# Another order of one attention step on four engines, a null key padded to 128 rows, and a VectorE copy of half of the mixed heads

## The reference, cut to what matters

```python
q = (xn @ Wq).reshape(b, n, HEADS, DIM_HEAD).transpose(0, 2, 1, 3)   # 16 heads of 64
kv = xn @ Wkv                                                       # one key and value for all heads
k = jnp.concatenate([nk, k], axis=1)                                # a null key in front: 129 keys
v = jnp.concatenate([nv, v], axis=1)
q = l2norm(q) * q_scale
k = l2norm(k) * k_scale
sim = jnp.einsum('bhid,bjd->bhij', q, k) * SCALE
sim = sim + attn_bias                                               # relative position and null bias
sim = jnp.where(causal, neg, sim)
attn = jax.nn.softmax(sim, axis=-1)
out = jnp.einsum('bhij,bjd->bhid', attn, v)
out = out.transpose(0, 2, 1, 3).reshape(b, n, HEADS * DIM_HEAD)
return ln(out @ Wout, g_out)
```

## Time and profile before

| what | value |
|---|---|
| median of 3 runs | 434.51 us |
| profiled execution, own time | 434.13 us |
| its span, first to last instruction | 432.0 us |
| busy share of the span, PE / DVE / ACT / POOL | 83% / 68% / 65% / 53% |
| mean granted TensorE clock | 0.929 |
| chain that ended last, by engine | PE 60%, DVE 16%, POOL 7%, issue 7%, ACT 5%, DMA 4% |
| attention steps 3 to 15 | 81 us to 231 us of the span |

### The profile page before, as it was taken

How to read it: one execution, slowest core, us unless ns; L and a number is a source line. 1 busy time by engine, 2 the same in 40 slices (tenths; PEclk the granted TensorE clock), 3 DMA queues, 4 the chain that set the end, 5 groups by cost and what they waited for, 6 DMA issues and landing times.

```text
span 432.0 us, 10178 instructions
## 1 busy us (share of the span) xinstructions
PE 357.3 (83%) x2921; PEld 295.1 (68%) x2922; DVE 292.6 (68%) x1144; ACT 279.5 (65%) x935; POOL 229.2 (53%) x253
## 2 busy tenths in 40 slices
PE   0286776999999999999998989697619999999980
PEld 0275655677777777777776648496519999999980
DVE  1848385888888888888889894757305565566545
ACT  1385594999999999999996773464304444444440
POOL 5024843678876667667872552277730444344420
PEclk9998995999999999999999687869958999999997
DMA  6726299990000000000000000011121222111117
GB/s 185 204 80 200 67 212 191 202 163 2 2 2 2 3 2 2 3 0 2 3 2 2 1 2 0 14 50 58 49 56 26 63 61 61 49 56 55 35 58 236
DMA packets 39479, 26.55 MB, mean 61 GB/s; under 512 B 4464, under 2 KB 37130, under 8 KB 39438
## 3 DMA queue, kind: packets, MB, share of 16 engines
q1 hardware_dynamic: 34256, 20.60, 21.8%
q0 software_dynamic: 2240, 4.23, 2.9%
q10 hardware_dynamic: 2942, 1.21, 1.1%
HBM read 12.89 MB, written 13.54 MB: 61 GB/s over the span
## 4 chain that ended last, share of the span: by engine, by line
PE 60%; DVE 16%; POOL 7%; issue 7%; ACT 5%; DMA 4%; SPq 1%; ACTq 0%; DVEq 0%; POOLq 0%
PE bank L1188 45%; PE bank L1185 14%; POOL sent_rows L537 7%; DVE p_space L1014 2%; ACT p_space L687 2%; DMA q_space<-in_L_cond_g_dram 2%; DVE biasm_space L1140 1%; DVE xn L934 1%; DMA bias<-result_rows 1%; DVE low L1018 1%; DVE p_space L841 1%; ACT xn L610 1%; DVE GL L918 1%; ACT yh L779 1%; DVE norm_in L812 1%
## 5 line engine op out<-in xcount | busy, mean ns | idle before, releaser
L687 ACT ACTIVATE p_space<-p_space,low 128x129 f32<-128x129 f32 x256 | 99.0, 391 | 6.4 <-DVE low L1018 6.4
L502 POOL TENSOR_TENSOR p_space<-p_space,inv 128x516 f32<-128x516 f32 x64 | 67.1, 1049 | 66.1 <-DVE inv L1026 66.1
L1014 DVE SCALAR_TENSOR_TENSOR p_space<-bank,rn,biasm_space 128x129 f32<-128x129 f32 x256 | 72.0, 343 | 22.3 <-PE bank L1188 22.0
L493 POOL TENSOR_TENSOR biasm_space<-bias,madd 128x516 f32<-128x516 f32 x64 | 75.6, 1192 | 7.4 <-DVE p_space L1014 7.3
L543 POOL DMA_INDIRECT result_rows<-oT_space,dest_ring x38 | 37.6, 990 | 60.8 <-DVE dest_ring L1154 60.1
L768 ACT ACTIVATE biasm_space<-bank 128x384 f32<-128x384 f32 x54 | 26.6, 492 | 58.1 <-PE bank L1185 58.0
L1185 PE MATMUL bank<-ident,p_space 128*128 128x128 f32 (+1 forms) x272 | 48.5, 297 | 2.4 <-POOL p_space L502 2.1
L687 ACT ACTIVATION_READ_ACCUMULATOR p_space<-p_space,low 128x1 f32 x256 | 48.5, 190 | 0.0
L1188 PE MATMUL bank<-DT,biasm_space 128*128 (+1 forms) x324 | 46.4, 281 | 1.2 <-ACT biasm_space L768 1.2
L702 ACT ACTIVATE pT<-bank 128x512 f32<-128x512 f32 x64 | 37.3, 583 | 13.9 <-PE bank L1188 12.8
L1018 DVE TENSOR_REDUCE low<-p_space 128x4 f32<-128x516 f32 x64 | 44.2, 691 | 2.2
(11 more groups left out here) (217 smaller groups left out, 705.4 us busy)
## 6 DMA issues: line engine op xcount, KB each, us to landing
sent_rows<-fill_row SPq DMA_DIRECT2D x2, 1950.0 KB, 24.1
sent_rows<-fill_row SPq DMA_DIRECT2D x2, 1885.0 KB, 19.6
q_space<-sent_rows SPq DMA_DIRECT2D x38, 65.0 KB, 1.9
xs<-in_x_dram SPq DMA_DIRECT2D x4, 256.0 KB, 6.3
bias<-bias_rows SPq DMA_DIRECT2D x1, 1024.0 KB, 5.8
xn<-result_rows SPq DMA_DIRECT2D x4, 256.0 KB, 4.4
bias<-result_rows SPq DMA_DIRECT2D x4, 256.0 KB, 5.6
out_dram<-xs SPq DMA_DIRECT2D x4, 256.0 KB, 2.5
```

Source lines behind the costliest of these rows:

```text
L493: nc.gpsimd.tensor_tensor(biasm[:, b % 2, heads, :], bias[:, heads, :], madd[:, b:b + 1, :].to_broadcast([P, HC, KEYS]), ALU.add).then_inc ...
L502: nc.gpsimd.tensor_tensor(v, v, spread(inv[:, b % 2, heads], KEYS), ALU.mult).then_inc(p_normed, 1)
L687: last = nc.scalar.activation(v, v, ACT.Exp, bias=low[:, b % 2, h:h + 1], accum_out=den[:, b % 2, h:h + 1])
L1014: last = nc.vector.scalar_tensor_tensor(Pb[:, q, h, :], src, rn[:, q, h:h + 1], biasm[:, q, h, :], ALU.mult, ALU.add)
```

## The change

Six edits. (1) TensorE's step has another order: `mix(2)` moves to the next step, in front of `mix(3, 3)`; `scores(3)` follows `scores(2)`; `turn_pn` goes in front of `turn_p(3)`, and `turn_sums` comes last. (2) The first half of the mixed heads is copied by VectorE, a new `keep_oT` between `invert(1, 1)` and `scores(3)`; ScalarE keeps the second half. The semaphore `oT_kept` becomes `oT0_kept` and `oT1_kept`. (3) ScalarE's `keep_q(1)` goes in front of `keep_pT(1)`, and `keep_pn` in front of `keep_pT(3)`. (4) VectorE's `invert(3, 2)` goes in front of `scores(1)`. (5) GpSimd's step has another order, and chunks 2 and 3 of the masked bias are made for batches t and t-1 instead of t-2. (6) `null_out` and `pnT` have 128 rows, zeroed by two memsets at the start, so that the null key's matmul contracts over 128 rows.

The diff, without the declarations of semaphores and tiles (and with the calls in the steps):

```diff
@@ gpsimd @@
+            nc.gpsimd.memset(null_out[:, :], 0.0).then_inc(const_made, 1)
+            nc.gpsimd.memset(pnT[:, :], 0.0).then_inc(const_made, 1)
...
                 norm_p(2, 3)
-                add_mask(2, 2)
+                norm_p(3, 3)
+                norm_p(0, 2)
                 add_mask(0, 0)
-                norm_p(3, 3)
-                add_mask(3, 2)
-                norm_p(0, 2)
+                norm_p(1, 2)
+                add_mask(3, 1)
+                add_mask(2, 0)
                 add_mask(1, 0)
-                norm_p(1, 2)
@@ scalar @@
-                        nc.scalar.activation(pnT[:, :], bank[4][0:H, 0:P][:, ::-1], ACT.Copy).then_inc(pn_kept, 1)
+                        nc.scalar.activation(pnT[0:H, :], bank[4][0:H, 0:P][:, ::-1], ACT.Copy).then_inc(pn_kept, 1)
...
-                def keep_oT(g, back):
-                    if on(back):
-                        b = t - back
-                        act.wait_ge(mixed, NCH * b + 2 * (g + 1))
+                def keep_oT():
+                    if on(3):
+                        b = t - 3
+                        act.wait_ge(mixed, NCH * b + 4)
                         need(act, y_made, b - 1)
...
-                keep_oT(1, 3)
+                keep_oT()
...
+                keep_q(1)
                 keep_pT(1)
-                keep_q(1)
...
-                keep_oT(0, 2)
+                keep_pn()
                 keep_pT(3)
-                keep_pn()
@@ vector @@
+                def keep_oT():
+                    if on(2):
+                        b = t - 2
+                        dve.wait_ge(mixed, NCH * b + 2)
+                        need(dve, y_made, b - 1)
+                        nc.vector.tensor_copy(oT[:, p, 0:HALF * P].rearrange("p (k s) -> p k s", k=HALF),
+                                              bank[6][:, :].rearrange("p (k s) -> p k s", k=HALF)[:, :, ::-1]).then_inc(oT0_kept, 1)
...
                 scores(0)
+                invert(3, 2)
                 scores(1)
-                invert(3, 2)
...
+                keep_oT()
                 scores(3)
@@ tensor @@
                         if c % 2 == 0:
-                            need(pe, oT_kept, 2 * b + c // 2)
+                            need(pe, oT1_kept if c == 0 else oT0_kept, b + c // 2)
...
-                        pe.wait_ge(oT_kept, 2 * (t - 2))
+                        pe.wait_ge(oT0_kept, t - 2)
+                        pe.wait_ge(oT1_kept, t - 2)
...
                 queries(0)
                 turn_p(0)
+                mix(2, 3)
                 mix(3, 3)
...
                 scores(2, 1)
+                scores(3, 1)
                 mix(1, 2)
                 sum_squares()
...
+                turn_pn()
                 turn_p(3)
-                scores(3, 1)
                 turn_sums()
...
-                turn_pn()
-                mix(2, 2)
```

More of the change, by code:

```diff
@@ L50, in adaln_ffn_kernel @@
     CHAIN = 11
-    CONSTS = 23
+    CONSTS = 25
     MLP0_DMAS, MLP_DMAS, ROW_DMAS, SCALE_DMAS, EXPERT_DMAS = 3, 5, 3, 5, 5
@@ L113, in adaln_ffn_kernel @@
         vsel = sb("vsel", [P, QT, H])
-        null_out = sb("null_out", [H, D])
+        null_out = sb("null_out", [P, D])
         bias = sb("bias", [P, H, KEYS])
@@ L155, in adaln_ffn_kernel @@
         pT = sb("pT", [P, 2, HC * P])
-        pnT = sb("pnT", [H, P])
+        pnT = sb("pnT", [P, P])
         o_space = sb("o_space", [P, 2 * HD])
@@ L247, in adaln_ffn_kernel @@
             "biasm_made", "scored", "biased", "maxed", "exped", "inv_made", "p_normed"))
-        p_turned, p_kept, pn_turned, pn_kept, mixed, oT_kept, y_made, y_kept = (sem(n) for n in (
-            "p_turned", "p_kept", "pn_turned", "pn_kept", "mixed", "oT_kept", "y_made", "y_kept"))
+        p_turned, p_kept, pn_turned, pn_kept, mixed, oT0_kept, oT1_kept, y_made, y_kept = (sem(n) for n in (
+            "p_turned", "p_kept", "pn_turned", "pn_kept", "mixed", "oT0_kept", "oT1_kept", "y_made", "y_kept"))
         yh_made, yl_made, gate_made, up_made, silu_made, h_made, h_turned, hT_kept, down_made, down_kept, fin_made = (
@@ L649, in _ @@
             act.wait_ge(null_turned, 1)
-            nc.scalar.activation(null_out[:, :], bank[7][0:H, 0:D], ACT.Copy).then_inc(null_kept, 1)
+            nc.scalar.activation(null_out[0:H, :], bank[7][0:H, 0:D], ACT.Copy).then_inc(null_kept, 1)
             def keep_yT(g):
@@ L707, in keep_sums @@
                         nc.scalar.activation(sums_sb[:, :], bank[7][:, 0:P], ACT.Copy).then_inc(sums_kept, 1)
-                def keep_oT(g, back):
-                    if on(back):
-                        b = t - back
-                        act.wait_ge(mixed, NCH * b + 2 * (g + 1))
+                def keep_oT():
+                    if on(3):
+                        b = t - 3
+                        act.wait_ge(mixed, NCH * b + 4)
                         need(act, y_made, b - 1)
-                        nc.scalar.activation(oT[:, b % 2, g * HALF * P:(g + 1) * HALF * P].rearrange("p (k s) -> p k s", k=HALF),
-                                             bank[6][:, :].rearrange("p (k s) -> p k s", k=HALF)[:, :, ::-1], ACT.Copy).then_inc(oT_kept, 1)
+                        nc.scalar.activation(oT[:, q, HALF * P:2 * HALF * P].rearrange("p (k s) -> p k s", k=HALF),
+                                             bank[6][:, :].rearrange("p (k s) -> p k s", k=HALF)[:, :, ::-1], ACT.Copy).then_inc(oT1_kept, 1)
                 if t == NB + 1:
@@ L1433, in step @@
                     expert_across(LATE[3])
-                turn_pn()
-                mix(2, 2)
             run_steps(pe, step)
-            pe.wait_ge(oT_kept, 2 * NB)
+            pe.wait_ge(oT0_kept, NB)
+            pe.wait_ge(oT1_kept, NB)
             expert_regs = [pe.alloc_register(f"expert_reg{k}") for k in range(RING + 2)]
```

## The result

| what | before | after |
|---|---|---|
| median of the timed runs | 434.25 us | 446.16 us |
| ratio, with its 95% interval | | 1.028 [1.025, 1.031] |
| profiled execution, own time | 434.13 us | 446.81 us |
| its span | 432.0 us | 445.0 us |
| one middle step, from `project` to `project` | 12.04 us | 12.75 us |

The account below looks back on a forecast made before the run. The prediction took TensorE to bound the kernel before, and VectorE with GpSimd after. Holds, the copy and the end summed to +17.3 us on 434.13, giving 451 us, range 438 to 464.

Parts of the forecast that it names:

- The mechanism: In `norms`, VectorE links with two SBUF inputs starting inside GpSimd's adds wait for the pass: two or three of about 1.1 us per step.
- The walk: Timing from the start of invert(1,1) in a middle step: GpSimd's adds end at 5.03 us, holding the norm chain 1.85 us.
- TensorE's pause: Before `project` in each middle step, TensorE waits about 1.7 us for VectorE's norm result.
- VectorE's step: Middle steps: 10.4 us plus 0.6 copy plus 1.85 hold, about 12.8 us, bounds 12.55 and 13.2.
- The copy: The copy moved to VectorE adds 0.6 us of work, with no wait in a full step.
- TensorE at 11.1 us: Middle steps: six fewer changes of matmul shape at 0.16 us each, so TensorE needs 11.1 us instead of 12.04.
- The clock rival: TensorE's granted clock falls in the new pauses of the middle steps: 465 us, or part of it, chance 0.18.
- The rival that the holds do not decide: The schedule drifts until GpSimd's adds miss the links, and TensorE's gain of 0.95 us per step counts: 424 us, chance 0.10.
- The rival of one hold per step: One held link per step instead of two and a half, VectorE's step 12.0 us: about 438 us, chance 0.12.
- The early steps: Steps 0, 1 and 2: holds, plus the copy in step 2, add 1.9, 3.0 and 2.2 us.
- The end: Step 14's root for y gains 0.9 us; step 17's `choose`, behind the VectorE copy, costs 2.0 us.
- The root's -0.9: In step 14 one GpSimd add no longer runs beside the root for y, saving 0.9 us.

Follow-up runs that it names:

- experiment 1: The changed kernel with GpSimd's order of before put back: 424.15 us, ratio 0.978.
- experiment 4: The changed kernel with two `add_mask` passes instead of three between GpSimd's norm passes of chunks 1 and 2: 434.38 us, ratio 1.003.
- experiment 9: The changed kernel with one `add_mask` pass between those norm passes and the other adds placed to wait for nothing late: 424.38 us, ratio 0.975.
- experiment 6: The changed kernel with the norm chain's handed-on values in PSUM and two products per Newton step swapped: 418.35 us, ratio 0.964.
- experiment 3: The changed kernel with both copies of the mixed heads on ScalarE, none on VectorE: 442.02 us, ratio 1.023.
- experiment 8: The kernel before with the null key padded to 128 rows and nothing else: 428.28 us, ratio 0.988.
- experiment 2: The kernel before with GpSimd's new order alone: 451.09 us, ratio 1.043.
- experiment 10: The changed kernel with the norm chain's values in PSUM and step 17's first-half copy on ScalarE: 415.16 us, ratio 0.956.
- experiment 11: The changed kernel with the norm chain's values in PSUM, step 17's first-half copy on ScalarE and GpSimd's order of before: 417.19 us, ratio 0.960.
- experiment 5: The changed kernel with two `add_mask` passes moved behind GpSimd's norm pass of chunk 3, leaving one behind that of chunk 1: 444.12 us, ratio 1.024.
- experiment 7: The changed kernel with GpSimd's order of before and, in step 17 alone, the first-half copy on ScalarE: 419.40 us, ratio 0.967.

## Why the prediction was right

It said 451 us (438 to 464), slower at 0.79; the measured 446.16 lies in the range and beyond 2%, and at the low edge of the forecast's own 446 to 456. By its steps:

- **The mechanism** was right and is shown: links that start inside GpSimd's adds, two per step at 1.11 us. The walk gave a hold of 1.85, the trace has 1.88; it had the first exposed link delayed by 0.04 and two held fully, and so it is. TensorE's pause came to 1.42 us, where 1.7 was said. Experiments 1, 4 and 9 move the adds away one by one and the hold goes with them; experiment 6 leaves them and takes away the SBUF operand.
- **VectorE's step**: 12.8 predicted, 12.75 measured; steps 3 to 14 +9.1 against +8.97.
- **The copy** at 0.6: it holds VectorE 0.58 (175.36 to 175.94), with no wait ahead of it in a full step, and experiment 3 shows that its length does not count while the adds set the end.
- **TensorE** at 11.1 us: 11.09 in experiment 1, and 0.17 per change of shape in experiment 8.
- **The clock rival** (465): the granted clock stayed at 1.00 in the middle step. TensorE pauses 1.42 us of 12.75 there, and that did not lower it. At the end it did fall: it was 0.50 (1.2 GHz) from 281.0 to 284.5 us, while TensorE waited for `choose`, and from 285.0 to 292.5, where the 16 matmuls of `project` of step 18 took 3.75 us, against 2.05 at 1.00 before. The sum had no term for it. The wait is not shown to be the cause: in experiment 3 `choose` starts in time, and this `project` takes 3.75 us too.
- **The rival that the holds do not decide** (424): that is the step of experiment 1, at 424.15. That the whole agrees so well is luck, since its end came out otherwise (`project` of step 18 16.81 us behind that of step 17, against 12.94 before, where +2.0 was said). **The rival of one hold per step** (438): experiment 4 has one, at 434.38.

The sum was too high by 4.6 us (+17.3 against +12.7 between the profiled executions). Two of its terms were mis-sized, and the start, +0.88 where the sum had 0, happened to take back part of it:

- **The early steps**, +7.1 in the sum, +5.18 in the table. The holds themselves were right (step 0 +1.95; step 1's chain from its first link to `low_expert` 6.16 against 3.25, +2.91 for +3.0). What the sum left out is that `scores(3)` of step 1 no longer waits for TensorE (0.91 us; it is so in experiments 1 and 3 too, which have TensorE's new order, and not in 2, which has the old one), and that in step 2 the norms were not the last thing before: their last link ended at 85.16, and `project` began at 86.57, behind TensorE's own work. These 1.4 us took up part of the hold.
- **The end**, +1.1 in the sum, -2.35 in the table. The root's -0.9 was right (its twelve instructions take 3.31 us against 4.25). Missing were the scalings of y, 1.81 us instead of 2.71 because add2 no longer runs beside them (as experiments 10 and 11 show), and the logits, 2.74 us instead of 3.51, since the granted clock fell later. The rows are 262:266 before and 275:279 after, both with TensorE busy throughout:

```profile
262.00:266.00 4.00, 4.00 (x32) 3.76 (x30) 0.58 (x3) 0.00 (x0) 0.73 (x1) 0.90 0.00 0
```

```profile
275.00:279.00 4.00, 4.00 (x38) 3.90 (x36) 0.58 (x3) 0.00 (x0) 0.70 (x1) 1.00 0.01 4
```

The way from the logits to the ranks, with `choose` behind the copy, grew by 1.35, not 2.0. That the clock falls later here was seen, not tested.

As for the start, the first norm link starts between 50.84 and 53.39 us in the fourteen profiled executions of this study, with the two memsets at 51.11 (experiment 3) and at 53.39 (experiment 1), without them at 50.84 (experiment 2) and at 51.92 (before), so no part of it can be given to the change.

## What to carry to other kernels

A chain of small dependent VectorE instructions with two SBUF inputs each needs a stretch in which GpSimd is silent; an order that fills GpSimd's idle time can cost the whole gain of the other engines, so look at what the other engine does in an idle gap before filling it. Where the values that its links hand on can lie in PSUM, it ran beside GpSimd unharmed here, and GpSimd's order no longer set the length of the middle steps (experiments 10 and 11). When an instruction is moved, look for what it waits for at its new place (experiments 2 and 5), and look at the first and last steps of a pipeline by themselves (experiment 7).

## What was not expected of the hardware

- Not only links with two SBUF inputs are held. L943 in experiment 10, a TENSOR_SCALAR of 128x12 with one tensor input in SBUF, takes 1.05 us beside norm2 (and 0.17 for 128x4 at 261.77, with no `norm_p` or `add_mask` beside it), and the four scalings of 128x128 (L948) take 1.82 or 2.71 us by what GpSimd does beside them: singly 0.32 to 0.34 us, or 1.07 and 1.23 where a pass holds them. The same section of the Trainium skill's page "SBUF — State Buffer" counts `tensor_scalar` among the operations that can run in a two-port mode and then contend with GpSimd; the trace agrees with its 1.05 us. A TENSOR_SCALAR that reads PSUM (L1057) kept its 0.17 inside the first add.
- A link in PSUM is no slower than one in SBUF at this size: 0.17 to 0.18 us for 128x16.
